# Local attention on one Trainium2 core: rotary partner rows fetched by DMA, 64-row score matmuls, and the exponentials of each head on ScalarE from PSUM

## The chip, the cores and the metric

The kernel runs as one launch on 1 core of one Trainium2 chip, all in float32. The metric is the device time of the launch in microseconds (us). The engines of the core are named PE (TensorE), ACT (ScalarE), DVE (VectorE), POOL (GpSimd) and SP (SyncE, which here only issues DMAs). Each runs its own list of instructions in order; the lists are tied together by semaphores only.

## The reference

The program is two transformer layers over x of shape (2, 2048, 128): local attention, a mixture of experts, causal attention and a second mixture of experts, each with a layer norm and a residual. Only the first stage is touched by the change:

```python
xn = rmsnorm(layernorm(x), norm_w)
q, k, v = split(xn @ w_qkv)              # 16 heads of 64
q, k = rope(q), rope(k)                  # x*cos + x_rot*sin; x_rot: (-x[odd], x[even]) of each pair
# segments of 64 tokens; 16 memory keys/values (pm_k, pm_v) are put before the 64 of the segment
scores = q_s @ k_s.T * 64**-0.5          # per head 64 x 80
scores = where(allowed, scores, min)     # memory, and causal inside the segment
attn = softmax(scores)
out = (attn @ v_s) @ w_out + b_out
x = x + layernorm(out)
```

## The kernel before, in words

The stage `local_attention` (L88) first loads x and the weights and splits every weight into a high float32r part `wh` and a low part `wl` (`matmul_split`, L62, computes a product as three matmuls: high·high at L64, high·low at L65, low·high at L66). The rotated weight columns (`rot`, the odd/even partners with their sign) are prepared once as weights of their own, so that the projection yields both x and x_rot.

The work is cut in 16 **steps** (`NSUB`). A step projects one block b of 256 tokens and at the same time attends over the block before, a, as two tiles of 128 tokens (s = 0, 1); the function `step` is written out for each engine, and the order of its lines is the order on that engine. A loop (`Fori`, L300) runs the middle steps in pairs. A last step has only the attention of the last block.

- PE, per step: values of b (`values_of`, four products of 512 columns, L64 to L66), then 16 column tiles ct (`project`, eight for q and eight for k, each with two products, one plain and one rotated, of 256 columns) in two PSUM banks `pbank`. Between them stand the scores of tile (a, 1) (`scores`, L535: per bank two mask matmuls at L542 and up to six pairs of 160 columns at L547; the keys of a head pair lie in one 160-column tile `kt` of 128 rows, with zeros where a head's rows meet the other's columns), and the **fills** of both tiles: seven PSUM fills per tile (`FILL`), transposes of the probabilities ("pt", L595) and products with the values ("ot", L603), alternating between two banks `fbank`, each copied out by ACT (L499). Then the output product (L616, L619). At the end of the step come the scores of tile (b, 0) and the transpose of the next block's input (`turn`, L529).
- ACT: four value copies (L506), one exponential per tile over all 16 heads, SBUF to SBUF (L490), the 14 fill copies (L499), the high part of the next input (`high`, L484).
- DVE: low part of the input (`low`, L322); per tile three maxima (L348), three subtractions of the maximum out of PSUM (L355), and after the exponential the sum (L363), its reciprocal (L365) and half of the normalising product (L369); 16 products with cos and sin straight from `pbank` (`rope`, L339), eight additions for the upper half of the keys (L330); the layer norm of the output (L376 to L391).
- POOL: the other additions of cos and sin part (L439 for q, L442 for k), the other half of the normalising product (L451, L454), a power per tile (L461).

What orders the stage are these lists and the waits in them: `project(ct)` waits until DVE has read tile ct-2 out of its bank, `scores` until DVE has subtracted in the bank, a fill until the normalised probabilities are there and until the bank's last copy is done.

## Time and profile before

| | |
|---|---|
| time, median of 3 runs | 2588.97 us (2580.05 to 2591.15) |
| profiled execution | 2589.86 us, its span 2588.0 us |
| granted clock of PE, mean over the span | 0.938 of full speed |
| busy: PE, PE weight loads, DVE, ACT, POOL | 87%, 66%, 67%, 36%, 17% of the span |
| local attention, in the trace | start to about 658 us |

The profile is one execution.
### The profile page before, as it was taken

How to read it: one execution, taken by the hardware profiler on the slowest of the kernel's cores; microseconds unless marked ns; L12 is line 12 of the kernel's file. 1: busy time of each engine (PE TensorE's matmuls, PEld its weight loads, DVE VectorE, ACT ScalarE, POOL GpSimd, SP SyncE). 2: the span in 40 equal slices, each digit the busy share in tenths (PEclk: the TensorE clock that was granted, in tenths of full speed). 3: DMA queues.
4: the chain of work that ended last, by engine and by line, in shares of the span. 5: the costliest groups of instructions: out<-in, count | busy, mean ns of one | idle time of the engine just before them, and what ended most of it. 6: DMA issues, size and time to landing. Idle time of an engine off the chain costs nothing. (4 is left out here: it accounts for less than half of the span.)

```text
span 2588.0 us, 42404 instructions
## 1 busy us (share of the span) xinstructions
PE 2258.5 (87%) x14360; PEld 1708.4 (66%) x14360; DVE 1726.0 (67%) x4490; ACT 930.4 (36%) x1496; POOL 452.8 (17%) x426
## 2 busy tenths in 40 slices
PE   4999999998499998999976887699778969999998
PEld 3878888887244443444445776488657867888887
DVE  6888888887666664666647777767677775453334
ACT  2333333333135453444442221223223324444443
POOL 4655655564200000000000000300020010000000
PEclk9999999999589998899988998799889979999999
DMA  3000000000100000000000000000000010000000
GB/s 120 2 1 0 0 0 0 0 1 1 34 1 1 1 1 1 1 1 1 1 0 1 0 0 14 26 1 1 2 1 1 1 75 1 4 8 4 4 4 8
DMA packets 14259, 20.85 MB, mean 8 GB/s; under 512 B 1984, under 2 KB 12864, under 8 KB 13376
## 3 DMA queue, kind: packets, MB, share of 16 engines
q1 hardware_dynamic: 14144, 19.37, 2.2%
q8 instruction: 66, 1.08, 0.2%
q14 instruction: 49, 0.40, 0.1%
HBM read 17.27 MB, written 2.10 MB: 7 GB/s over the span
## 5 line engine op out<-in xcount | busy, mean ns | idle before, releaser
L974 ACT ACTIVATE mb_pt<-mb_stb 128x1024 f32<-128x1024 f32 x256 | 248.2, 1023 | 235.7 <-PE mb_stb L1063 235.0
L880 DVE TENSOR_REDUCE mb_mxp<-mb_p1b 128x1 f32<-128x512 f32 x352 | 225.6, 682 | 91.9 <-PE mb_p1b L1047 91.9
L2233 PEld LDWEIGHTS md_bk<-md_w,md_a 128*128 128x128 f32 x2048 | 263.9, 192 | 27.9 <-ACT md_a L2080 4.8
L2233 PE MATMUL md_bk<-md_w,md_a 128*128 128x128 f32 x2048 | 268.0, 276 | 4.0 <-DVE md_acc L2177 2.7
L2080 ACT ACTIVATE md_a<-md_bk,md_b 128x512 f32<-128x512 f32 x256 | 175.5, 687 | 240.5 <-PE md_bk L66 240.2
L1073 PE MATMUL mb_pvb<-mb_pt,mb_v 128*33 128x512 f32 x1024 | 244.4, 599 | 0.0
L2177 DVE SCALAR_TENSOR_TENSOR md_acc<-md_bk,md_gate,md_acc 128x128 f32<-128x128 f32 x256 | 71.7, 343 | 232.0 <-PE md_bk L2233 231.8
L339 DVE TENSOR_TENSOR ma_tr<-ma_pbank,ma_cs 128x512 f32<-128x512 f32 x256 | 173.5, 688 | 70.4 <-PE ma_pbank L66 65.8
L64 PE MATMUL ma_pbank<-ma_xth,ma_wh 128*128 128x256 f32 x512 | 165.2, 323 | 3.9 <-DVE ma_tr L339 1.9
L1856 ACT ACTIVATE mc_p<-mc_sb,mc_nb 128x512 f32<-128x512 f32 (+3 forms) x160 | 97.9, 621 | 190.2 <-DVE mc_nb L1744 190.2
L499 ACT ACTIVATE ma_pt<-ma_fbank 128x512 f32<-128x512 f32 (+1 forms) x160 | 85.3, 553 | 211.2 <-PE ma_fbank L595 211.2
L1934 PE MATMUL mc_pv<-mc_v,mc_pt 128*128 128x128 f32 x1088 | 150.3, 282 | 11.5 <-DVE mc_pt L1793 11.3
L1934 PEld LDWEIGHTS mc_pv<-mc_v,mc_pt 128*128 128x128 f32 x1088 | 134.3, 192 | 22.9 <-DVE mc_pt L1793 18.5
L1063 PE MATMUL mb_stb<-mb_qs,mb_ks 98*128 98x512 f32 x512 | 145.5, 406 | 3.2 <-ACT mb_pt L974 1.6
L65 PE MATMUL ma_pbank<-ma_xth,ma_wl 128*128 128x256 f32 x512 | 143.2, 280 | 0.0
L66 PE MATMUL ma_pbank<-ma_xtl,ma_wh 128*128 128x256 f32 x512 | 143.1, 279 | 0.0
L1047 PE MATMUL mb_p1b<-mb_ks,mb_qs 96*128 96x512 f32 x352 | 137.2, 473 | 2.8 <-DVE mb_qs L873 2.8
L64 PE MATMUL md_bk<-md_nh,md_wh 128*128 x256 | 120.4, 470 | 15.1 <-DVE md_acc L2177 12.4
L1047 PEld LDWEIGHTS mb_p1b<-mb_ks,mb_qs 96*128 96x128 f32 x352 | 63.6, 200 | 104.0 <-DVE mb_mxp L880 84.8
L442 POOL TENSOR_TENSOR ma_kt<-ma_tr 64x256 f32<-64x256 f32 x128 | 118.5, 930 | 54.5 <-DVE ma_tr L339 54.3
L1063 PEld LDWEIGHTS mb_stb<-mb_qs,mb_ks 98*128 98x128 f32 x512 | 94.9, 192 | 48.9 <-issue 13.4
L1184 POOL TENSOR_TENSOR mb2a_r<-mb2a_sv,mb_half 128x16 f32<-128x16 f32 x2 | 5.8, 2898 | 681.5 <-DVE mb2a_sv L1213 681.5
(333 smaller groups left out, 4956.0 us busy)
## 6 DMA issues: line engine op xcount, KB each, us to landing
mg_X<-x SPq DMA_DIRECT2D x4, 512.0 KB, 10.7
ma_cs<-cs SPq DMA_DIRECT2D x1, 2048.0 KB, 10.1
mc_cs<-cs SPq DMA_DIRECT2D x1, 2048.0 KB, 7.9
md_raw<-d_w SPq DMA_DIRECT2D x1, 2048.0 KB, 7.4
md_w<-d_w SPq DMA_DIRECT2D x1, 2048.0 KB, 10.9
out<-mg_X SPq DMA_DIRECT2D x8, 256.0 KB, 2.3
ma_raw<-w_qkv SPq DMA_DIRECT2D x1, 1536.0 KB, 8.8
mb_r<-b_w SPq DMA_DIRECT2D x1, 1152.0 KB, 5.2
```

What stands on the lines that cost most here:

```text
L64: nc.tensor.matmul(out, lhs_hi, rhs_hi, start=start, stop=False)
L65: nc.tensor.matmul(out, lhs_lo, rhs_hi, start=False, stop=False)
L66: return nc.tensor.matmul(out, lhs_hi, rhs_lo, start=False, stop=stop)
L339: nc.vector.tensor_tensor(tr[:, ct % 4, :, :], pbank[:, ct % 2, :].rearrange("p (r c) -> p r c", r=2), cs[:, bass.ds(b.j, 1), :, :].rearra ...
L880: nc.vector.tensor_reduce(mxp[:, r // NCH, r % NCH:r % NCH + 1], pass_bank(r), AXX, ALU.max).then_inc(p1_max, 1)
L974: nc.scalar.activation(pt[:, i % RING, :, :], stb[:, 2 * (i % 2):2 * (i % 2) + 2, :], ACT.Exp, scale=float(SCALE_B)).then_inc(exp_done, 1)
L1047: nc.tensor.matmul(pass_bank(r), qs[V % 2][0:QROWS, hh, t * P:(t + 1) * P], ks[0:QROWS, c * BLK:(c + 1) * BLK], start=True, stop=True).the ...
L1063: last = nc.tensor.matmul(stb[:, 2 * (i % 2) + hh, :], ks[:, i * P:(i + 1) * P], qs[U % 2][:, hh, :], start=True, stop=True)
L1073: last = nc.tensor.matmul(pvb[64 * hh:64 * hh + DK + 1, :], v1[:, i, :], pt[:, i % RING, hh, :], start=(i == 0), stop=(i == KT - 1), skip_ ...
L1934: last = nc.tensor.matmul(pv[:, 0:D], pt[:, k % 2, a * P:(a + 1) * P], v[:, c * BPT + a, :], start=(c == 0 and a == 0), stop=(c == chunks[ ...
L2080: nc.scalar.activation(a[:, e % 2, c, :], ub[:, c, :], ACT.Gelu, bias=b1[:, e, c:c + 1]).then_inc(gelu, 1)
L2233: last = nc.tensor.matmul(db[:, e % 2, s * P:(s + 1) * P], a[:, e % 2, c, s * P:(s + 1) * P], w2[:, e, c, :], start=(c == 0), stop=(c == F ...
```

## The change

It rewrites the stage in these places:

1. **Rotary partners by DMA.** The rotated weights and their projections are gone: 8 groups of two plain column tiles per step remain (`project`). ACT copies each group from `pbank` to SBUF (`copy_out`), SP issues two DMAs per group that write each row's partner row (odd to even, even to odd) to `swp`, DVE multiplies the copy by cos (`cosine`) and the partner by a signed sin (`sine`), both from SBUF, and POOL adds two column tiles at once over all 128 rows (`add`).
2. **64-row scores.** The keys of a head lie on 64 rows with 80 columns. A score matmul has 64 rows, 64 columns of queries and 80 of keys; there are two groups (j = 0, 1) of 8 heads per tile in four PSUM banks, 4 mask matmuls and 16 score matmuls for each group.
3. **Exponentials.** DVE takes two negated maxima per tile (640 columns each); ACT computes each head's exponential straight from PSUM with the negated maximum as bias, 16 instructions of 80 columns per tile. The six subtractions are gone. The scale is folded into the q weights.
4. **Order.** The loop is written out, a tile's seven fills of s = 1 stand together behind the last projection, and `turn` and the output product share the two `fbank` banks, so `turn` is last in the step.

```diff
-            srcs = [(raw, 0, 0), (rot, 0, 2), (raw, 1024, 0), (rot, 1024, 0), (raw, 2048, 0)]
...
+            @block.sync
+            def _(sp):
+                for G in range(NSUB * NG):
+                    r = G % RAWS
+                    sp.wait_ge(raw_ready, G + 1)
+                    if G >= RAWS:
+                        sp.wait_ge(rope_sin, G - RAWS + 1)
+                    for i in range(2):
+                        sp.dma_start(swp[i:P:2, r, :, :], raw[1 - i:P:2, r, :, :]).then_inc(swapped[r], 16)
...
+                def cosine(b, i):
+                    G = b * NG + i
+                    dve.wait_ge(raw_ready, G + 1)
+                    if G >= TRS:
+                        dve.wait_ge(rope_add, G - TRS + 1)
+                    nc.vector.tensor_tensor(tr[:, G % TRS, 0, :, :], raw[:, G % RAWS, :, :],
+                                            cs[:, b // 2, 0, None, :].to_broadcast([P, 2, SUB]),
+                                            ALU.mult).then_inc(rope_cos, 1)
...
-                def tile_sub(a, s, b3):
...
+                def maxes(a, s, j):
+                    dve.wait_ge(s_mm, (a * ST + s) * QUADS + j + 1)
+                    nc.vector.tensor_reduce(mx[:, s, 8 * j:8 * j + 8].rearrange("p (b i) -> p b i", b=2), bank_of(j),
+                                            AXX, ALU.max, negate=True).then_inc(s_max, 1)
...
-                            nc.scalar.activation(e[:, s, :, :], e[:, s, :, :], ACT.Exp, scale=SCALE0).then_inc(exp_done, 1)
...
+                def exps(a, s):
+                    for j in range(QUADS):
+                        act.wait_ge(s_max, (a * ST + s) * QUADS + j + 1)
+                        for k in range(8):
+                            slot = 8 * j + k
+                            nc.scalar.activation(e[:, s, slot, :],
+                                                 sbank[:, 2 * j + k // 4, k % 4 * KEYS0:(k % 4 + 1) * KEYS0], ACT.Exp,
+                                                 bias=mx[:, s, slot:slot + 1]).then_inc(exp_done, 1)
...
+                    if live:
+                        values(b, 0, 1, 2, 3)
+                        copy_out(b, 0)
+                    if old:
+                        exps(a, 0)
+                    if live:
+                        copy_out(b, 1, 2)
+                    if old:
+                        exps(a, 1)
+                        evacuate(a, 0, 0, 1)
+                    if live:
+                        copy_out(b, 3)
+                    if old:
+                        evacuate(a, 0, 2, 3)
...
+                def scores(b, s, j):
+                    T = b * ST + s
+                    if T > 0:
+                        pe.wait_ge(exp_done, (T - 1) * H0 + 8 * j + 8)
+                    if s == 0:
+                        pe.wait_ge(rope_add, b * NG + (4 if j == 0 else 8))
...
+                    for i in range(4):
+                        for hf in range(2):
+                            q0 = s * P + 64 * hf
+                            for rg in range(2):
+                                rows, half = slice(64 * rg, 64 * rg + 64), slice(64 * hf, 64 * hf + 64)
+                                last = nc.tensor.matmul(sbank[half, 2 * j + rg, i * KEYS0:(i + 1) * KEYS0],
+                                                        qt[rows, par(b), 4 * j + i, q0:q0 + 64],
+                                                        kt[rows, par(b), 4 * j + i, 2 * s + hf, :],
+                                                        start=False, stop=True, skip_group_check=True)
```

How the instructions stand on three engines before and after (names: `ma_pbank` projections, `ma_qk` their copy in SBUF, `ma_swp` the partner rows, `ma_sbank` scores, `ma_e` exponentials, `ma_fbank` fills, `ma_pt`/`ma_ot` their copies).

ACT, the start of a step, before (second step of the program):

```order
L506 ACTIVATE ma_v<-ma_pbank 128x512 x4
L490 ACTIVATE ma_e<-ma_e 128x1280
L499 ACTIVATE ma_pt<-ma_fbank 128x512 x2
L490 ACTIVATE ma_e<-ma_e 128x1280
L499 ACTIVATE ma_ot<-ma_fbank 128x512
L499 ACTIVATE ma_pt<-ma_fbank 128x512 x2
```

and the same place in the changed kernel (third step):

```order
L501 ACTIVATE ma_v<-ma_pbank 128x512 x4
L511 ACTIVATE ma_qk<-ma_pbank 128x512
L483 ACTIVATE ma_e<-ma_sbank,ma_mx 128x80 x16
L511 ACTIVATE ma_qk<-ma_pbank 128x512 x2
L483 ACTIVATE ma_e<-ma_sbank,ma_mx 128x80 x16
L494 ACTIVATE ma_pt<-ma_fbank 128x512 x2
L511 ACTIVATE ma_qk<-ma_pbank 128x512
L494 ACTIVATE ma_ot<-ma_fbank 128x512
```

The first exponentials now stand behind a copy of the step's own projection, and the second 16 stand ahead of the first two fill copies, which in the kernel before stood ahead of the second exponential.

DVE, the start of a step, before:

```order
L322 TENSOR_TENSOR ma_xtl<-ma_misc,ma_xth 128x256
L348 TENSOR_REDUCE ma_mx<-ma_sbank 128x6 x2
L348 TENSOR_REDUCE ma_mx<-ma_sbank 128x4
L355 TENSOR_TENSOR ma_e<-ma_sbank,ma_mx 128x480 x2
L355 TENSOR_TENSOR ma_e<-ma_sbank,ma_mx 128x320
L339 TENSOR_TENSOR ma_tr<-ma_pbank,ma_cs 128x512
L363 TENSOR_REDUCE ma_den<-ma_e 128x16
L365 RECIPROCAL ma_rden<-ma_den 128x16
L369 TENSOR_TENSOR ma_pb<-ma_e,ma_rden 64x16x64
L339 TENSOR_TENSOR ma_tr<-ma_pbank,ma_cs 128x512 x4
```

and in the changed kernel:

```order
L314 TENSOR_TENSOR ma_xtl<-ma_fbank,ma_xth 128x256
L338 TENSOR_REDUCE ma_mx<-ma_sbank 128x8 x2
L322 TENSOR_TENSOR ma_tr<-ma_qk,ma_cs 128x512
L344 TENSOR_REDUCE ma_den<-ma_e 128x16
L346 RECIPROCAL ma_rden<-ma_den 128x16
L350 TENSOR_TENSOR ma_pb<-ma_e,ma_rden 64x16x64
L322 TENSOR_TENSOR ma_tr<-ma_qk,ma_cs 128x512
L329 TENSOR_TENSOR ma_tr<-ma_swp,ma_cs 128x512
L338 TENSOR_REDUCE ma_mx<-ma_sbank 128x8 x2
```

The sum and product of the first tile (L344 to L350) stand ahead of the maxima of the second (the last row), with one cosine and one sine between them.

PE, the end of a step in the changed kernel, behind the last projection:

```order
L623 MATMUL ma_fbank<-mg_ident,ma_pb 128x128 x8
L631 MATMUL ma_fbank<-ma_pt,ma_v 64x128 x8
L623 MATMUL ma_fbank<-mg_ident,ma_pb 128x128 x8
L631 MATMUL ma_fbank<-ma_pt,ma_v 64x128 x8
L623 MATMUL ma_fbank<-mg_ident,ma_ppm 128x128 x2
L640 MATMUL ma_fbank<-ma_wout,ma_ot 128x128 x8
L643 MATMUL ma_fbank<-ma_pmvw,ma_pt 128x128 x2
L593 MATMUL ma_sbank<-ma_mask,mg_identb 64x320 x4
L600 MATMUL ma_sbank<-ma_kt,ma_qt 64x80 x16
```

No projection is left between these fills; before, tiles 12 to 15 of `project` stood between them, and `turn` stood ahead of the last two score banks instead of behind all scores.

## Rows read from the trace of the kernel before

**Rows 1.** Busy us (instructions) by window: PE, PEld, DVE, ACT, POOL; then granted clock.
```profile
248.20:285.90 37.70, 36.05 (x328) 30.53 (x330) 31.06 (x58) 12.71 (x22) 21.29 (x22) 1.00 0.00 0
587.00:662.00 75.00, 56.73 (x526) 48.17 (x522) 48.70 (x109) 22.63 (x37) 29.56 (x30) 0.93 0.03 7
```
**Rows 2.** Timeline of ACT: L484 ten steps apart, two fill copies. Start us, us.
```profile
97.66 0.38 ACT L484 ACTIVATE ma_xth<-ma_misc 128x256 fp32r<-128x256 f32 x1 [3.48 <-PE ma_misc L529]
...
262.19 1.09 ACT L499 ACTIVATE ma_pt<-ma_fbank 128x512 f32<-128x512 f32 x2 [7.14 <-PE ma_fbank L595]
...
474.16 0.38 ACT L484 ACTIVATE ma_xth<-ma_misc 128x256 fp32r<-128x256 f32 x1 [3.90 <-PE ma_misc L529]
```
**Rows 3.** Timeline of PE, start of a middle step.
```profile
249.94 0.50 PE L64 MATMUL ma_pbank<-ma_wh,ma_xth 128*128 128x512 f32 x1
...
253.25 0.39 PE L64 MATMUL ma_pbank<-ma_xth,ma_wh 128*128 128x256 f32 x1
...
254.15 0.39 PE L542 MATMUL ma_sbank<-ma_mask,mg_identb 128*64 128x480 bf16 x2
254.38 0.98 PE L547 MATMUL ma_sbank<-ma_kt,ma_qt 128*64 128x160 f32 x12
...
261.55 1.03 PE L595 MATMUL ma_fbank<-mg_ident,ma_pb 128*128 128x128 f32 x8
```
**Rows 4.** Timeline, end of a middle step: next input's high and low part.
```profile
285.88 0.38 ACT L484 ACTIVATE ma_xth<-ma_misc 128x256 fp32r<-128x256 f32 x1 [3.91 <-PE ma_misc L529]
...
286.34 0.42 DVE L322 TENSOR_TENSOR ma_xtl<-ma_misc,ma_xth 128x256 fp32r<-128x256 f32 x1
```
**Rows 5.** Groups by line and shape: count, busy us, mean ns.
```profile
L499 ACT ACTIVATE ma_pt<-ma_fbank 128x512 f32<-128x512 f32 x128 | 73.0, 596 | 195.8 <-PE ma_fbank L595 195.8
L499 ACT ACTIVATE ma_pt<-ma_fbank 128x256 f32<-128x256 f32 x32 | 12.3, 384 | 15.4 <-PE ma_fbank L595 15.4
L1856 ACT ACTIVATE mc_p<-mc_sb,mc_nb 128x512 f32<-128x512 f32 x112 | 75.9, 684 | 170.5 <-DVE mc_nb L1744 170.5
L348 DVE TENSOR_REDUCE ma_mx<-ma_sbank 128x6 f32<-128x480 f32 x64 | 38.9, 647 | 0.3 <-PE ma_sbank L547 0.3
L348 DVE TENSOR_REDUCE ma_mx<-ma_sbank 128x4 f32<-128x320 f32 x32 | 15.3, 480 | 0.0
```
**Rows 6.** Timeline, softmax of one tile on DVE and POOL in a middle step.
```profile
254.45 0.69 DVE L339 TENSOR_TENSOR ma_tr<-ma_pbank,ma_cs 128x512 f32<-128x512 f32 x1 [1.96 <-PE ma_pbank L66]
255.08 1.49 DVE L363 TENSOR_REDUCE ma_den<-ma_e 128x16 f32<-128x1280 f32 x1
...
256.89 1.22 DVE L369 TENSOR_TENSOR ma_pb<-ma_e,ma_rden 64x1024 f32<-64x1024 f32 x1
256.94 2.94 POOL L451 TENSOR_TENSOR ma_pb<-ma_e,ma_rden 64x1024 f32<-64x1024 f32 x1 [0.98 <-DVE ma_rden L365]
```
**Rows 7.** Timeline of the causal attention: DVE and POOL, both reading SBUF.
```profile
1640.97 1.30 POOL L1814 TENSOR_TENSOR mc_rp<-mc_tr 128x512 f32<-128x512 f32 x1 [0.68 <-DVE mc_tr L1704]
1640.99 1.83 DVE L1710 TENSOR_TENSOR mc_kql<-mc_rp,mc_kqh 128x512 fp32r<-128x512 f32 x1
...
1643.87 0.67 DVE L1710 TENSOR_TENSOR mc_kql<-mc_rp,mc_kqh 128x512 fp32r<-128x512 f32 x1
```
**Rows 8.** Timeline of PE, last step, which has no projections.
```profile
635.03 1.97 PE L595 MATMUL ma_fbank<-mg_ident,ma_pb 128*128 128x128 f32 x8 [4.76 <-POOL ma_ppm L454]
...
646.32 1.04 PE L595 MATMUL ma_fbank<-mg_ident,ma_pb 128*128 128x128 f32 x8
648.18 1.09 PE L603 MATMUL ma_fbank<-ma_pt,ma_v 128*64 128x128 f32 x16 [0.83 <-ACT ma_pt L499]
...
653.27 2.02 PE L616 MATMUL ma_misc<-ma_wout,ma_ot 128*128 128x128 f32 x16 [0.41 <-ACT ma_ot L499]
655.13 0.61 PE L619 MATMUL ma_misc<-ma_pmvw,ma_pt 128*128 128x128 f32 x4
```
**Rows 9.** DMA issues: KB each, median us from issue to landing.
```profile
mg_X<-x SPq DMA_DIRECT2D x4, 512.0 KB, 10.7
...
mc_wo<-c_wo SPq DMA_DIRECT2D x1, 128.0 KB, 2.4
```

More of the change, by code:

```diff
@@ L432, in _ @@
+                finish(NSUB - 1, 1)
             @block.gpsimd
             def _(pool):
[L434 to L465 removed]
@@ L516, in step @@
                         high(nxt)
-                high(Sub(0, 0))
-                steps(act, step)
             @block.tensor
@@ new lines, in project @@
+                def project(b, i):
+                    if i >= 2:
+                        pe.wait_ge(raw_ready, b * NG + i - 1)
+                    else:
+                        pe.wait_ge(v_copied, b * 2 * ST + 3 + i)
+                    kind, c = GROUPS[i]
+                    for half in range(2):
+                        w0 = (1024 if kind == "k" else 0) + (2 * c + half) * P
+                        last = matmul_split(nc, pbank[:, i % 2, half * SUB:(half + 1) * SUB], wh[:, w0:w0 + P],
+                                            wl[:, w0:w0 + P], xth[:, :], xtl[:, :])
+                    last.then_inc(proj_mm, 1)
@@ L585, in fill @@
+                    last.then_inc(s_mm, 1)
+                def fill(a, s, *fills):
+                    T = a * ST + s
+                    for i in fills:
                         kind, q = FILL[i]
-                        bank = fbank[:, (s * FILLS + i) % 2, :]
+                        bank = fbank[:, i % 2, :]
                         if i == 0:
@@ new lines, in _ @@
+                turn(0)
+                for b, a, nxt in steps:
+                    live, old = b is not None, a is not None
+                    if live:
+                        values_of(b)
+                        project(b, 0)
+                    if old:
+                        scores(a, 1, 0)
+                    if live:
+                        project(b, 1)
+                    if old:
+                        scores(a, 1, 1)
+                    if live:
+                        project(b, 2)
+                    if old:
+                        fill(a, 0, 0, 1)
+                    if live:
+                        project(b, 3)
+                    if old:
+                        fill(a, 0, 2, 3)
+                    if live:
+                        project(b, 4)
+                    if old:
+                        fill(a, 0, 4, 5)
+                    if live:
+                        project(b, 5)
+                    if old:
+                        fill(a, 0, 6)
+                    if live:
+                        project(b, 6)
+                    if old:
+                        out_project(a, 0)
+                    if live:
+                        project(b, 7)
+                    if old:
+                        fill(a, 1, *range(FILLS))
+                        out_project(a, 1)
+                    if live:
@@ L655, in step @@
                         scores(b, 0, 0)
-                    if nxt:
-                        if a:
-                            pe.wait_ge(y_read, (a.n + 1) * ST)
+                        scores(b, 0, 1)
+                    if nxt is not None:
                         turn(nxt)
-                    if b:
-                        scores(b, 0, 1)
-                        scores(b, 0, 2)
-                turn(Sub(0, 0))
-                steps(pe, step)
 class Stats:
```

543 lines of the change are left out of this document (240 added, 303 removed).

## The prediction

> **What bounds the kernel now.** I read the busy time by windows first. In one middle step of local attention PE is busy for 36.05 of 37.70 us at a granted clock of 1.00 (2.4 GHz); DVE for 31.06, POOL for 21.29, ACT for 12.71 [rows 1]. Two starts of the same ACT instruction ten steps apart, 97.66 and 474.16, give the step: 37.65 us [rows 2]. So the stage is bound by PE's work, and DVE, though 82% busy, ends second. Then the timeline of PE at the start of a step: values 3.3 us, one projection 0.9 us, a bank of scores about 1.15 us with its masks, and the first fill 11.6 us into the step without a wait [rows 3]: whatever softmax needs is hidden under six projections. Last the timeline of the final step, which has no projections: there the fills of a tile and its output product are a chain of PE and ACT in turns [rows 8].
>
> **What the work alone would give.** 8 of 16 projections go, about 0.8 us each in a stream: -6.4 us of PE per step. PE's list is then: values 3.3, projections 6.8, fills and output products 11.8, `turn` 0.4, scores 4 groups. A group is 32 records of matmuls with 64 columns of weights and 4 masks. The nearest row with the same weights is L603: 16 records in about 1.03 us, 64 ns each [rows 8]; L547 has 76 ns for 160 columns [rows 3]. With its two column halves running together, one such record holds its half for 152 ns, so 80 columns for 76 ns. Upper end, nothing overlapping: 32 x 76 ns + 0.5 for the masks = 2.9 us. Lower end, all four quarters at once: 32 x 19 ns + 0.2 = 0.8 us. I take 1.8 us, nearer to L603 (32 x 64 ns + 0.25 = 2.3). Then PE's work is 29.5 us, against 34.5 by the same count before. DVE loses the subtractions and upper-half additions; ACT gains. If work decided, the step would fall. I do not think it will, since the order of the lists makes a longer chain of waits than 37.65 us.
>
> The Trainium skill ("TensorE: Matmul & The Clock Gate", Part 3) says that matmuls in different row and column tiles run concurrently and that weight loads overlap them only where the row group differs. By that rule a group costs the 0.8 us of the lower end, and the chain below is 2.0 us shorter per step. No row here has matmuls on separate 64-row halves; L547 shows the column halves overlapping.
>
> **The chain of a middle step, from PE's first value product at 0.** Ends without and with the port conflict told below.
> - Values 3.3, projection 0 0.9 [rows 3], 0.3 until its result can be read (254.15 to 254.45) [rows 3, 6], copy by ACT 0.6 [rows 5]: 5.1 us.
> - 16 exponentials of tile 0. They are ready earlier (their maxima need only DVE at 0 to 1.6 us) but stand behind the copy on ACT. One: 596 ns for 512 columns and 384 for 256 give 0.83 ns a column, so 238 ns for 80, and 88 ns more for the bias from memory (684 against 596) [rows 5]; two in a row overlap by 0.10 us (1.09 for two) [rows 2]. So 226 ns each, 3.7 us: 8.8 us. Ends: 0.14 us each without the bias cost, 0.33 without overlap, that is -1.4 and +1.6 us per tile. One instruction of 1.27 us did this before.
> - Sum, reciprocal (1.81 us to the next) and half product 1.26 on DVE [rows 6]: 11.9 us. All 16 heads must be there.
> - One cosine and one sine, 0.60 each behind one another (0.67 recorded [rows 7]): 13.1 us; with the conflict 15.0.
> - First negated maximum of tile 1: 647 ns for 480 columns and 1.04 ns for each of 160 more [rows 5]: 0.8 us: 13.9 / 15.8.
> - 16 exponentials of tile 1: 3.7: 17.6 / 19.5. Behind them on ACT wait the two fill copies of tile 0, 1.1 us [rows 2]: 18.7 / 20.6. PE's fills 0 and 1 can be there from 14.3 us (POOL's product ends 2.94 + 0.6 after the reciprocal [rows 6]); PE does projection 3 and then has nothing.
> - From the second copy to the output product of tile 0: ot 1.05, pt 0.4, projection 0.85, 0.3 to its result, its copy 0.5, copy of pt 0.6, hop 0.1, ot 1.05, projection 0.8, pt 0.15, projection 0.8: 6.6 us: 25.3 / 27.2.
> - Output product 2.2 (653.27 to 655.13 and the last four records 0.36 behind), projection 7 0.8: 28.3 / 30.2.
> - Fills and output product of tile 1, now without projections between them: the last step before shows the same chain from 646.32 to 655.74, 9.4 us at full clock [rows 8]: 37.7 / 39.6.
> - Scores of the next tile, two groups: 3.6: 41.3 / 43.2. The additions of the last group, on POOL at about 37 to 40 us, are in time.
> - `turn` 0.4, then with nothing on PE behind it the high part on ACT and low part on DVE, 285.88 to 286.76 and hops, 1.05 [rows 4]: 42.75 / 44.65 us.
>
> **The port conflict.** In the causal attention a DVE product of two SBUF operands took 1.83 us where POOL had begun an addition from SBUF 0.02 us before it, and 0.67 us where it had not [rows 7]; the blocked one ended 0.55 us after POOL's. Before, `rope` read PSUM and ran freely; cosine and sine read two SBUF operands, 16 per step. The first cosine that counts is issued at 11.9 us, inside POOL's product of about 10.65 to 13.6 us, so it ends near 14.15 and the sine near 15.0: +1.9 us. Later conflicts fall beside PE's own work. I take the 1.9 in full; the other end is 0.
>
> The Trainium skill ("SBUF — State Buffer", Who interferes with whom) states this rule: a DVE instruction with two SBUF inputs and a GpSimd instruction that reads SBUF exclude one another for a whole instruction. By it the step is the second number, without it the first; the rows above agree with it.
>
> **The clock.** After 4.76 us of idle time PE did eight transposes in 1.97 us instead of 1.04, at the 1.2 GHz level, and the window of the last steps has 0.93 [rows 8, 1]. The changed step has idle times of about 2.8 us (the wait for the exponentials ahead of the scores), 1.5 and 2.4 to 4.3 us (ahead of ot). The work behind the last, 2.3 us on the chain, could double: 0 to +2.3 us, and a little at the other places. I take +1.0.
>
> **DMA.** 16 issues of 128 KB per step. A DMA of 128 KB landed 2.4 us after issue, four of 512 KB in a crowded queue 10.7 [rows 9]. The first sine is wanted 7 us after its copy, the last about 5: hidden below some 5 us, and at 10.7 each step would wait some 5 us more. I take 0.
>
> **The rest at nothing:** the subtractions and the key additions lay beside PE, so removing them gains nothing here; two weight parts fewer in the preparation lie beside the loading of constants; the first and the last step I leave as they are, within 3 us.
>
> **The sum.** 44.65 + 1.0 = 45.65 us per step, 8.0 more than 37.65. Fifteen steps have both halves: +120 us on the profiled 2589.9 (2588.0 of span and 1.9 around it), 2709.9, which stands 0.9 above the median of the runs shown. Forecast 2710 us.
>
> **Rivals.**
> - *The short chain* (score groups 0.8, no conflict, full clock): 42.75 - 2.0 = 40.75 us, +46 us, 2636. For it: the exponentials' overlap and column halves that run together. Against: rows 7. Still slower. With exponentials at 0.14 us the step would reach 38.0.
> - *The clock falls widely, or transfers arrive late*: 49 to 51 us a step, 2760 to 2790. For it: three idle times per step where there was none. Against: 29.5 us of work in 45.
> - *PE's work stays the bound*: if the waits on ACT and DVE overlap better than I walked them, the step is PE's 29.5 us and the 3.15 that step and count differed by before, 32.65 us: -75 us, 2514. It decides only where the chain falls below 37.65, that is where softmax of tile 0 is through before the fills are wanted and tile 1's exponentials don't hold up the fill copies. Against: the order on ACT is fixed in the lists.
> - *The parts cancel*: near 2589.
>
> Chances: forecast with its bounds 0.62, short chain 0.20, wide clock or late DMA 0.11, PE's work 0.05, cancelled 0.02. Slower by over 0.5% (13 us, about what a measurement of this kernel tells from no change) 0.93, within 0.03, faster 0.04. The range leaves out the faster cases and the far ends: 2645 to 2775 us, from a step of 41.3 to one of 50.
>
> **What would show it.** A step of 43 to 47 us between two high-part copies. ACT's exponentials about 0.23 us apart, 3.7 us per tile, and the two fill copies directly behind the second 16. PE waiting 2 us and more at L600's masks, at the first pt and at the first ot, the last ended by ACT. DVE's cosine at 1.2 to 1.9 us where POOL's product runs. About 9.4 us from the eight transposes to the end of the output product. PE's busy share below 75% and a granted clock below 1.00. It is wrong if the step is below 41 us, if the score groups take over 2.5 us, or if PE waits for the partner rows.

## The result and the profile after

The changed kernel takes 2690.9 us (median of 4 runs, 2689.8 to 2691.4), the kernel before beside it 2588.3; the ratio is 1.0401, 95% interval 1.0377 to 1.0425: slower by 102.6 us. The profiled execution has a span of 2688.6 us and a mean granted clock of 0.901, where it was 0.938. PE's busy share over the program fell from 87 to 81%. In the medians below one execution is left out, of E3, which took 3248.9 us at a granted clock of 0.63.

By windows, one middle step of the changed kernel in three parts and whole, then the window of the last steps (columns: us, busy time and instructions of each engine, granted clock, DMA share, GB/s):

```profile
core 0: us, PE busy (x) PEld busy (x) DVE busy (x) ACT busy (x) POOL busy (x), PEclk, DMA share, GB/s
422.11:431.40 9.29, 5.92 (x60) 4.30 (x60) 3.12 (x6) 6.82 (x22) 0.00 (x0) 0.99 0.07 28
431.40:449.19 17.79, 10.97 (x88) 9.34 (x87) 14.05 (x15) 8.67 (x26) 10.23 (x6) 0.62 0.12 45
449.19:466.50 17.31, 14.93 (x200) 13.08 (x200) 11.80 (x21) 6.56 (x13) 9.46 (x9) 1.00 0.16 62
422.11:466.50 44.39, 31.82 (x346) 26.72 (x346) 28.97 (x41) 22.05 (x60) 19.69 (x14) 0.85 0.13 48
587.00:662.00 75.00, 53.92 (x609) 45.07 (x608) 47.30 (x72) 35.23 (x97) 30.78 (x23) 0.85 0.12 45
```

These answer to [rows 1]. PE had 96% of the step to do; now it is busy 72%, and no other engine is nearer to full. For 17.8 us of the step PE runs mostly at the lower of its clock levels.

The start of each step on ACT (start, duration), which answers to [rows 2]:

```profile
66.50 0.38 ACT L476 ACTIVATE ma_xth<-ma_fbank 128x256 fp32r<-128x256 f32 x1 [13.40 <-PE ma_fbank L555]
688.34 0.38 ACT L476 ACTIVATE ma_xth<-ma_fbank 128x256 fp32r<-128x256 f32 x1 [4.18 <-PE ma_fbank L555]
```

Fourteen steps lie between them: 44.42 us each (43.98 to 45.76), 6.77 more than 37.65. Over fifteen steps that is 101.5 us. That this is nearly the whole of the 102.6 us is partly chance, as two more rows show, the start of the second step before and the last matmuls of the stage after:

```profile
59.62 0.38 ACT L484 ACTIVATE ma_xth<-ma_misc 128x256 fp32r<-128x256 f32 x1 [20.73 <-PE ma_misc L529]
...
762.24 0.61 PE L643 MATMUL ma_fbank<-ma_pmvw,ma_pt 128*128 128x128 f32 x4
```

Up to the second step the changed kernel has lost 6.9 us (66.50 against 59.62), about half in the preparation and half in the first step, and its stage ends at 762.85 where it ended at 655.74 [rows 8], 107.1 us later. The code behind the stage, which nobody changed, was 6.5 us shorter in this execution (to the end of the span 1925.8 us, before 1932.3). In the traces of the experiments it takes 1924 to 1930 us, so differences of a few us in it say nothing.

The timeline of PE in the step that starts at 423.06 (start, us, in brackets the idle time ahead and what ended it), against [rows 3, 8]:

```profile
423.06 0.47 PE L64 MATMUL ma_pbank<-ma_wh,ma_xth 128*128 128x512 f32 x1 [0.98 <-ACT ma_xth L476]
...
429.74 0.33 PE L593 MATMUL ma_sbank<-ma_mask,mg_identb 64*64 64x320 bf16 x4 [2.43 <-ACT ma_e L483]
429.90 0.72 PE L600 MATMUL ma_sbank<-ma_kt,ma_qt 64*64 64x80 f32 x32
...
431.83 1.28 PE L600 MATMUL ma_sbank<-ma_kt,ma_qt 64*64 64x80 f32 x32
...
437.33 1.25 PE L623 MATMUL ma_fbank<-mg_ident,ma_pb 128*128 128x128 f32 x8 [2.64 <-POOL ma_ppm L446]
...
443.26 1.98 PE L631 MATMUL ma_fbank<-ma_pt,ma_v 128*64 128x128 f32 x16 [3.40 <-ACT ma_pt L494]
...
451.98 1.95 PE L640 MATMUL ma_fbank<-ma_wout,ma_ot 128*128 128x128 f32 x16
...
454.92 1.03 PE L623 MATMUL ma_fbank<-mg_ident,ma_pb 128*128 128x128 f32 x8
...
464.26 0.33 PE L593 MATMUL ma_sbank<-ma_mask,mg_identb 64*64 64x320 bf16 x4
...
465.77 0.44 PE L555 MATMUL ma_fbank<-mg_ident,ma_xn 128*128 128x128 f32 x2
```

The three long waits stand at the three places foretold, each ended by ACT or POOL. ACT in the same step:

```profile
427.84 3.59 ACT L483 ACTIVATE ma_e<-ma_sbank,ma_mx 128x80 f32<-128x80 f32 x16
...
438.59 3.60 ACT L483 ACTIVATE ma_e<-ma_sbank,ma_mx 128x80 f32<-128x80 f32 x16 [3.27 <-DVE ma_mx L338]
441.96 1.20 ACT L494 ACTIVATE ma_pt<-ma_fbank 128x512 f32<-128x512 f32 x2
```

Both fill copies stand directly behind the second sixteen exponentials, though PE had the fills ready at 438.3. And DVE and POOL between the two sets, to be held against [rows 6, 7]:

```profile
431.46 1.49 DVE L344 TENSOR_REDUCE ma_den<-ma_e 128x16 f32<-128x1280 f32 x1 [2.79 <-ACT ma_e L483]
...
433.27 1.22 DVE L350 TENSOR_TENSOR ma_pb<-ma_e,ma_rden 64x1024 f32<-64x1024 f32 x1
434.52 2.28 DVE L322 TENSOR_TENSOR ma_tr<-ma_qk,ma_cs 128x512 f32<-128x512 f32 x1
436.72 1.10 DVE L329 TENSOR_TENSOR ma_tr<-ma_swp,ma_cs 128x512 f32<-128x512 f32 x1
437.75 1.54 DVE L338 TENSOR_REDUCE ma_mx<-ma_sbank 128x8 f32<-128x640 f32 x2
439.21 0.68 DVE L322 TENSOR_TENSOR ma_tr<-ma_qk,ma_cs 128x512 f32<-128x512 f32 x1
```
```profile
433.31 2.94 POOL L443 TENSOR_TENSOR ma_pb<-ma_e,ma_rden 64x1024 f32<-64x1024 f32 x1 [11.42 <-DVE ma_rden L346]
436.21 1.06 POOL L446 TENSOR_TENSOR ma_ppm<-ma_e,ma_rden 128x256 f32<-128x256 f32 x1
```

A cosine takes 2.28 us beside POOL's product, and the next one 0.68 us where POOL is idle; cosine and sine each end about 0.55 us behind a POOL instruction. Last, the DMA issues (KB each, median us to landing; [rows 9]):

```profile
ma_swp<-ma_qk SPq DMA_DIRECT2D x256, 128.0 KB, 2.0
```

### The profile page after: what moved, and what is told of

The parts are those of the page before. It is cut to its first block and busy times, and to the rows that moved or that the text cites. A ratio compares the mean times of both kernels' runs of the same rounds, so it can differ in the third digit from the quotient of the medians.

```text
span 2688.6 us, 42307 instructions
## 1 busy us (share of the span) xinstructions
PE 2182.4 (81%) x14680; PEld 1644.4 (61%) x14680; DVE 1693.4 (63%) x4231; ACT 1070.6 (40%) x2102; POOL 426.0 (16%) x297
## 5 line engine op out<-in xcount | busy, mean ns | idle before, releaser
L322 DVE TENSOR_TENSOR ma_tr<-ma_qk,ma_cs 128x512 f32<-128x512 f32 x128 | 139.4, 1089 | 118.5 <-ACT ma_qk L511 118.0
L631 PE MATMUL ma_fbank<-ma_pt,ma_v 128*64 128x128 f32 x1024 | 85.6, 318 | 85.6 <-ACT ma_pt L494 85.6
L623 PE MATMUL ma_fbank<-mg_ident,ma_pb 128*128 128x128 f32 x512 | 97.9, 338 | 56.2 <-POOL ma_ppm L446 54.6
L483 ACT ACTIVATE ma_e<-ma_sbank,ma_mx 128x80 f32<-128x80 f32 x512 | 114.9, 379 | 68.2 <-DVE ma_mx L338 68.2
L631 PEld LDWEIGHTS ma_fbank<-ma_pt,ma_v 128*64 128x64 f32 x1024 | 69.1, 160 | 101.9 <-ACT ma_pt L494 101.9
L443 POOL TENSOR_TENSOR ma_pb<-ma_e,ma_rden 64x1024 f32<-64x1024 f32 x32 | 94.0, 2936 | 190.9 <-DVE ma_rden L346 190.9
L1096 PEld LDWEIGHTS mb_pvb<-mb_pt,mb_v 128*33 128x33 f32 x1024 | 49.0, 110 | 113.5 <-issue 113.2
```

Of the source, the lines that this page charges most:

```text
L322: nc.vector.tensor_tensor(tr[:, G % TRS, 0, :, :], raw[:, G % RAWS, :, :], cs[:, b // 2, 0, None, :].to_broadcast([P, 2, SUB]), ALU.mult). ...
L483: nc.scalar.activation(e[:, s, slot, :], sbank[:, 2 * j + k // 4, k % 4 * KEYS0:(k % 4 + 1) * KEYS0], ACT.Exp, bias=mx[:, s, slot:slot + 1 ...
L631: last = nc.tensor.matmul(bank[64 * hh:64 * hh + 64, (pr % 4) * P:(pr % 4 + 1) * P], v[:, par(a), s, h * DH0:(h + 1) * DH0], pt[:, slot_of ...
L1096: last = nc.tensor.matmul(pvb[64 * hh:64 * hh + DK + 1, :], v1[:, i, :], pt[:, i % RING, hh, :], start=(i == 0), stop=(i == KT - 1), skip_ ...
```

## The experiments

All times are medians, each with its own runs of the kernel before (2588.2 to 2589.6). "Against the changed kernel" compares the two differences from before; one step is a fifteenth of it.

**E1: the maxima of tile 1 first.**

```diff
                         softmax_back(a, 0)
+                        for j in range(QUADS):
+                            maxes(a, 1, j)
                     if live:
                         cosine(b, 1)
                         sine(b, 0)
-                    if old:
-                        for j in range(QUADS):
-                            maxes(a, 1, j)
```

> Edit on the changed kernel: on DVE the two maxima of tile 1 stand right behind softmax_back of tile 0, ahead of cosine 1 and sine 0; nothing else moves. Theory (the step is the chain through ACT's and DVE's lists): the blocked cosine (2.28 us) and sine (1.10) leave the chain, tile 1's 16 exponentials begin 3.3 us earlier, the fill copies behind them too; step 44.4 -> 41.1 us, 15 steps, -49 us, about 2642. Rival (the step is set by PE's work at the lower clock, or by something later in the step): the fills move but the step does not, within 10 us of 2691.

Measured: 2631.6 us, ratio to before 1.0159 (1.0142 to 1.0176), 60 us off the changed kernel. Its second sixteen exponentials start 13.3 us behind the high-part copy (405.36 less 392.10), where 438.59 less 422.11 is 16.5: 3.2 us earlier, 3.3 expected.

```profile
392.10 0.38 ACT L474 ACTIVATE ma_xth<-ma_fbank 128x256 fp32r<-128x256 f32 x1 [4.19 <-PE ma_fbank L553]
...
405.36 3.59 ACT L481 ACTIVATE ma_e<-ma_sbank,ma_mx 128x80 f32<-128x80 f32 x16
408.72 1.20 ACT L492 ACTIVATE ma_pt<-ma_fbank 128x512 f32<-128x512 f32 x2
```

Two instructions moved on an engine that is 65% busy are worth more than half of the loss; that engine's order is on the chain. The gain is 10 us above the forecast. The granted clock of such a step rose too, from 0.85 to 0.92; that it makes up the rest is not shown.

**E2: POOL's normalising products made tiny.**

```diff
-                    nc.gpsimd.tensor_tensor(pb[0:64, s, :, 0:SEG], e[0:64, s, :, PM:KEYS0],
+                    n, k = (H0, SEG) if a == 0 else (1, 1)
+                    nc.gpsimd.tensor_tensor(pb[0:64, s, 0:n, 0:k], e[0:64, s, 0:n, PM:PM + k],
...
```

> Edit on the changed kernel: from the second block on POOL's two normalising products per tile are made over 1 element a row (the lower half of the probabilities and the memory part keep the values of the first block; this part of the computation is left out). Port-conflict theory: cosine 1 and sine 0 behind the half product take 0.7 us each and end 2.0 us earlier; step -2.0 us, -30 us, about 2661. Rival (cosine is slow by itself, or from the partner DMAs that write SBUF at the same time): cosine 1 stays at 2.3 us, the time within 8 us of 2691.

Measured: 2661.8 us, ratio 1.0277 (1.0260 to 1.0294), 30 us off, as the conflict theory said. The edit takes away POOL's reading, its arithmetic and its writing together, so it names the product and not the part of it that shuts DVE out. DVE at the same place:

```profile
419.86 0.70 DVE L322 TENSOR_TENSOR ma_tr<-ma_qk,ma_cs 128x512 f32<-128x512 f32 x1
420.49 0.68 DVE L329 TENSOR_TENSOR ma_tr<-ma_swp,ma_cs 128x512 f32<-128x512 f32 x1
421.09 1.54 DVE L338 TENSOR_REDUCE ma_mx<-ma_sbank 128x8 f32<-128x640 f32 x2
```

**E3: exponentials without bias.**

```diff
-                                                 sbank[:, 2 * j + k // 4, k % 4 * KEYS0:(k % 4 + 1) * KEYS0], ACT.Exp,
-                                                 bias=mx[:, s, slot:slot + 1]).then_inc(exp_done, 1)
+                                                 sbank[:, 2 * j + k // 4, k % 4 * KEYS0:(k % 4 + 1) * KEYS0], ACT.Exp).then_inc(exp_done, 1)
```

> Edit on the changed kernel: the exponentials read no bias (the subtraction of the maximum is left out; the wait for the maxima stays). Theory from L1856's 684 against 596 ns: each exponential takes 0.14 us instead of 0.224, 16 take 2.3 us instead of 3.6; both tiles' are on the chain, so step -2.7 us, -40 us, about 2651. Rival: the fixed cost of a small ACT instruction out of PSUM is what counts, 0.22 us stays, and the time is within 8 us of 2691.

Measured: 2641.2 us, ratio 1.0197 (1.0168 to 1.0227), 51 us off (expected 40).

```profile
400.02 2.18 ACT L483 ACTIVATE ma_e<-ma_sbank 128x80 f32<-128x80 f32 x16
```

16 take 2.18 us, 0.136 us each, against 3.59 and 0.224: the bias read from SBUF costs 0.088 us each, 1.4 us a tile. Both tiles together explain 42 of the 51 us (15 steps of 2.8); the rest is open, and the granted clock over the middle steps rose beside it, from 0.85 to 0.88.

**E4: no partner DMAs.**

```diff
-                    nc.vector.tensor_tensor(tr[:, G % TRS, 1, :, :], swp[:, G % RAWS, :, :],
+                    nc.vector.tensor_tensor(tr[:, G % TRS, 1, :, :], raw[:, G % RAWS, :, :],
...
-                        sp.dma_start(swp[i:P:2, r, :, :], raw[1 - i:P:2, r, :, :]).then_inc(swapped[r], 16)
+                    sp.sem_inc(swapped[r], 32)
```

> Edit on the changed kernel: SP issues no DMAs for partner rows, the sine reads the copied rows themselves (the rotation is left out). Theory (transfers are hidden: 2.0 us from issue to landing, first wanted 7 us after the copy): within 5 us of 2691. Rival (late transfers or their SBUF writes hold up DVE): the sines start earlier or run faster, step -1 us or more, below 2676.

Measured: 2689.9 us, ratio 1.0387 (1.0368 to 1.0406): no difference from the changed kernel that could be told. The blocked cosine is as slow without any transfer beside it:

```profile
431.58 2.28 DVE L321 TENSOR_TENSOR ma_tr<-ma_qk,ma_cs 128x512 f32<-128x512 f32 x1
```

So the transfers are not its cause, and E2 has shown that POOL's products are.

**E5: turn ahead of the last output product.**

```diff
                         fill(a, 1, *range(FILLS))
-                        out_project(a, 1)
-                    if live:
-                        scores(b, 0, 0)
-                        scores(b, 0, 1)
                     if nxt is not None:
                         turn(nxt)
+                    if old:
+                        out_project(a, 1)
+                    if live:
+                        scores(b, 0, 0)
+                        scores(b, 0, 1)
```

> Edit on the changed kernel: on PE the transposes of the next block (turn) stand ahead of the output product and the scores that end the step, so that high and low part are made beside them. Chain theory: the 0.98 us in which PE waits for the low part goes, and nearly all of turn's place; step -1.0 to -1.4 us, 15 steps, -15 to -21 us, about 2673. Rival (the next step's start is held by ACT or DVE anyway): within 8 us of 2691.

Measured: 2674.9 us, ratio 1.0329 (1.0308 to 1.0351), 16 us off: 1.07 us a step. The wait of 0.98 us for the low part is gone; a new one of 0.59 us stands ahead of `turn`:

```profile
406.47 0.44 PE L555 MATMUL ma_fbank<-mg_ident,ma_xn 128*128 128x128 f32 x2 [0.59 <-ACT ma_pt L494]
```

**E6 and E9: needless matmuls in PE's waits.** E6 fills the first two waits, E9 all three. The cut below is E6's, but for its last two lines, which only E9 has: `spin_p` is the same as `spin` into `pbank`. E9 also has `spin(a, 5)` at the second place.

```diff
+                def spin(a, n):
+                    pe.wait_ge(y_read, a * ST)
+                    for _ in range(n):
+                        for half in range(2):
+                            matmul_split(nc, fbank[:, 1, half * SUB:(half + 1) * SUB], wh[:, 0:P], wl[:, 0:P],
+                                         xth[:, :], xtl[:, :])
...
                         project(b, 0)
+                    if live and old and a > 0:
+                        spin(a, 3)
                     if old:
                         scores(a, 1, 0)
...
                         project(b, 2)
+                    if live and old and a > 0:
+                        spin(a, 3)
...
                         project(b, 3)
+                    if live and old and a > 0:
+                        spin_p(b, 4)
```

> Edit on the changed kernel: in the two waits of PE ahead of the scores and ahead of the first fill (2.4 and 2.6 us) it makes three needless projections each (36 more matmuls a step) into a free bank; the result is the same and nothing waits for them. Clock theory (the granted clock fell to the 1.2 GHz level about 2 us after the first wait and the work from the fills to the first output product took 8.9 us where 6.6 was walked at full clock): with PE busy the clock stays at 1.00 there, step -2 us or more, -30 us, about 2660, faster although PE does more. Rival (the clock follows something else, or that work waits on ACT at either clock): the time stays at 2691 or rises.

Measured: 2690.6 us, ratio 1.0390 (1.0373 to 1.0407): nothing. The forecast of 2660 missed. The level no longer fell at the scores, but it fell at the fills, where PE had still waited 1.92 us, and stayed down through the products with the values:

```profile
392.59 1.69 PE L623 MATMUL ma_fbank<-mg_ident,ma_pb 128*128 128x128 f32 x8 [1.92 <-POOL ma_ppm L446]
...
398.54 1.97 PE L631 MATMUL ma_fbank<-ma_pt,ma_v 128*64 128x128 f32 x16 [2.98 <-ACT ma_pt L494]
```

So the null result left two readings open: that the clock costs nothing, or that the costly part was still slow. E9 was made to tell them apart.

> As e6, with five needless projections instead of three ahead of the first fill and four more (into the free projection bank) ahead of the first product with the values, where e6 still had PE idle for 1.9 and 3.0 us and the granted clock fell there: 72 needless matmuls a step. Clock theory: now the level stays at 2.4 GHz through the fills of tile 0; the eight projections and fills there take half the time they took, step -1 to -2.3 us, 2656 to 2676. Rival (the part between the fill copies and the output product waits for ACT's copies at either clock, and e6's null result says that the clock costs nothing here): within 8 us of 2691, or above it because the added matmuls stand in the way.

Measured: 2670.7 us, ratio 1.0316 (1.0299 to 1.0333): 72 more matmuls a step, and 20 us faster. The granted clock is 1.00 for the whole step, and the products with the values take 1.09 us instead of 1.98:

```profile
408.74:451.32 42.58, 36.12 (x418) 31.46 (x418) 29.95 (x41) 21.83 (x59) 20.12 (x14) 1.00 0.13 50
```
```profile
428.62 1.21 ACT L494 ACTIVATE ma_pt<-ma_fbank 128x512 f32<-128x512 f32 x2
...
429.92 1.09 PE L631 MATMUL ma_fbank<-ma_pt,ma_v 128*64 128x128 f32 x16 [1.31 <-ACT ma_pt L494]
...
436.37 1.95 PE L640 MATMUL ma_fbank<-ma_wout,ma_ot 128*128 128x128 f32 x16
...
440.48 0.66 PE L623 MATMUL ma_fbank<-mg_ident,ma_pb 128*128 128x128 f32 x4 [0.57 <-DVE ma_y L357]
```

From the second fill copy (429.83) to the output product (436.37) lie 6.5 us, where the changed kernel has 8.8 (443.16 to 451.98): 2.3 us less. 0.7 us of it is lost again behind it, where the second fill of tile 1 now waits for DVE.

**E7: one exponential per group.** One shift is shared by eight heads, which softmax allows as long as no head's scores lie so far below the others' that its exponentials vanish; a general kernel would need a guard.

```diff
-                        for k in range(8):
-                            slot = 8 * j + k
-                            nc.scalar.activation(e[:, s, slot, :],
-                                                 sbank[:, 2 * j + k // 4, k % 4 * KEYS0:(k % 4 + 1) * KEYS0], ACT.Exp,
-                                                 bias=mx[:, s, slot:slot + 1]).then_inc(exp_done, 1)
+                        nc.scalar.activation(e[:, s, 8 * j:8 * j + 8, :].rearrange("p (b i) k -> p b (i k)", b=2),
+                                             sbank[:, 2 * j:2 * j + 2, 0:QW], ACT.Exp,
+                                             bias=mx[:, s, j:j + 1]).then_inc(exp_done, 1)
```

> Edit on the changed kernel, order unchanged: one negated maximum over the 8 heads of a group and one exponential of 640 columns per group instead of 8 of 80 (4 per step instead of 32). Chain theory: 16 exponentials of 3.6 us become two of about 0.7 each, -2.2 us for each tile, both on the chain; step -4.4 us, -65 us, about 2626. Rival (only one of the two tiles is on the chain, the other is covered): -2.2 us a step, about 2658.

Measured: 2611.9 us, ratio 1.0087 (1.0070 to 1.0103), 79 us off (expected 65). The maxima are one for each group then, in an edit of the same kind that is not shown.

```profile
384.18 1.47 ACT L482 ACTIVATE ma_e<-ma_sbank,ma_mx 128x640 f32<-128x640 f32 x2
```

1.47 us for a tile in place of 3.59, and both tiles pay: 2.1 us twice in 15 steps is 64 of the 79 us. The mean granted clock rose from 0.901 to 0.916 beside it; what it is worth here was not measured.

**E12: part 3 alone, in the kernel before.**

```diff
-                            act.wait_ge(s_sub, (a.n * ST + s + 1) * 3)
-                            nc.scalar.activation(e[:, s, :, :], e[:, s, :, :], ACT.Exp, scale=SCALE0).then_inc(exp_done, 1)
+                            for b3 in range(3):
+                                h0, nh = 2 * PAIRS_OF_BANK[b3][0], 2 * len(PAIRS_OF_BANK[b3])
+                                act.wait_ge(s_max, (a.n * ST + s) * 3 + b3 + 1)
+                                for k in range(nh):
+                                    nc.scalar.activation(e[:, s, h0 + k, :],
+                                                         sbank[:, b3, k * KEYS0:(k + 1) * KEYS0], ACT.Exp,
+                                                         bias=mx[:, s, h0 + k:h0 + k + 1]).then_inc(exp_done, 1)
...
-                        pe.wait_ge(s_sub, (T - 1) * 3 + b3 + 1)
+                        pe.wait_ge(exp_done, (T - 1) * H0 + (6, 12, 16)[b3])
```

> The kernel before with the change's third part alone: negated maxima, no subtractions, 32 exponentials of 80 columns per step out of PSUM with bias, scale folded into the q weights; projections, rotation and scores as before. Theory (small exponentials on the chain cost here too: the scores of tile 1 wait for the first six of them, about 1.2 us, and the first fill, which had no slack, comes 1.5 us later; DVE has 2.9 us less to do): step 37.65 -> 39.5 to 40.5, 2615 to 2635. Rival (six projections and DVE's saved subtractions cover it): within 8 us of 2589.

Measured: 2638.0 us, ratio 1.0191 (1.0174 to 1.0208): 50 us slower, just above the theory's range. DVE is spared six subtractions a step and the kernel loses, with twice the projections there as cover. PE:

```profile
398.89 0.39 PE L536 MATMUL ma_sbank<-ma_mask,mg_identb 128*64 128x480 bf16 x2 [1.04 <-ACT ma_e L482]
...
404.86 0.38 PE L64 MATMUL ma_pbank<-ma_xth,ma_wh 128*128 128x256 f32 x1 [1.05 <-DVE ma_tr L340]
```

The scores wait for the exponentials as expected. What had not been walked is the second wait: on DVE the sum stands ahead of the next `rope`, so the late exponentials hold up the projections too.

**E8, E10, E11: the lists in another order.** E8 has E7's edit, and PE's list, written short, reads as in the second line in place of the first (ACT, DVE and POOL follow it):

```
-  p2 F0.0 F0.1 p3 F0.2 F0.3 p4 F0.4 F0.5 p5 F0.6 p6 O0 p7 | F1.0 to F1.6 O1 | S0 S1 turn
+  p2 F0.0 F0.1 p3 F0.2 F0.3 F0.4 p4 F0.5 F0.6 p5 O0 F1.0 p6 F1.1 p7 F1.2 F1.3 F1.4 S0 F1.5 F1.6 turn O1 S1
```

(p projections, Fs.i fill i of tile s, O output product, S the next block's scores.) ACT makes tile 0's exponentials around the first value copy; on DVE tile 0's sum comes ahead of cosine 0, and the maxima of tile 1 come right behind it, on either side of cosine 0. The first fill waits for POOL's first product alone.

```diff
-                            pe.wait_ge(p_norm, T * 2 + 2)
+                            pe.wait_ge(p_norm, T * 2 + 1)
...
+                        if i == FILLS - 1:
+                            pe.wait_ge(p_norm, T * 2 + 2)
...
-                        fill(a, 1, *range(FILLS))
-                        out_project(a, 1)
+                        fill(a, 1, 2, 3, 4)
                     if live:
                         scores(b, 0, 0)
+                    if old:
+                        fill(a, 1, 5, 6)
+                    if nxt is not None:
+                        turn(nxt)
+                    if old:
+                        out_project(a, 1)
+                    if live:
                         scores(b, 0, 1)
-                    if nxt is not None:
-                        turn(nxt)
```

> The changed kernel with e7's edit and with the lists of PE, ACT, DVE and POOL written in another order: tile 0's exponentials and softmax_back at the step's start ahead of values and cosines, both maxima of tile 1 behind them, the first fill waits only for the first normalising product, projections 5 to 7 between the fills of tile 1, scores of the next block inside them, turn ahead of the last output product. Chain theory (the cost of the change is the order of the lists; its PE work is 29.5 us a step): step 31 to 33 us, 15 steps, about -180 us, 2490 to 2530, faster than the kernel before. Rival (the waits between engines that the change adds, copy, partner DMA, small exponentials, keep the step above 37.65 in any order): 2590 or above.

Measured: 2561.7 us, ratio 0.9897 (0.9874 to 0.9919): faster than the kernel before, but a step of 35.85 us in place of 31 to 33. PE's largest wait:

```profile
412.91 0.97 PE L625 MATMUL ma_fbank<-mg_ident,ma_pb 128*128 128x128 f32 x4 [3.61 <-DVE ma_y L358]
```

The fill waits until DVE has read the output product, and that read stands on DVE behind a cosine and three sines that ran beside POOL's instructions and took 2.28, 1.10, 1.77 and 1.75 us.

E10 is E8 without E7's edit:

> e8's order of the lists, but with the changed kernel's own 32 exponentials of 80 columns and maxima per head: the reordering alone. Theory: of the 2.2 us per tile that e7's edit saved, tile 0's stays on the chain (its exponentials stand between the value copies and hold values and sum up by 1.9 us) and tile 1's is partly covered; step 36 -> 38.5 us, about 2600. Rival (in the new order the exponentials are covered): 2562 to 2575. Other end (both in full): 40.5, about 2630.

Measured: 2601.7 us, ratio 1.0048 (1.0031 to 1.0065). With every instruction of the change kept, the order, with the wait of the first fill that goes with it, gives back 89 of the 102.6 us.

E11 moves two things in E8. The lines that they are moved from, and the second value copy, which goes ahead of an exponential, are not shown:

```diff
-                    rot((cosine, 3), (sine, 2), (cosine, 4), (sine, 3), (cosine, 5), (sine, 4))
+                    rot((cosine, 3), (sine, 2), (cosine, 4))
                     if old:
                         out_read(a, 0)
-                    rot((cosine, 6), (sine, 5))
+                    rot((sine, 3), (cosine, 5), (sine, 4), (cosine, 6), (sine, 5))
...
                     rot((sine, 7), )
+                    if live:
+                        maxes(b, 0, 0)
...
                         high(nxt)
+                    if live:
+                        exps(b, 0, 0)
```

> e8 with two moves. DVE reads the output product of tile 0 (out_read) behind cosine 4, not behind sine 4; in e8 PE waited 3.6 us for that read ahead of the second fill of tile 1. The first maximum and the first exponential of the next tile 0 are made at the end of the step before, so that the value copies aren't held up (1.3 us). Theory: step 35.9 -> 32 to 33 us, about 2510. Rival (DVE, with its products shut out by POOL's, is the bound, and a read moved forward only pushes the rotations back, which the scores at the step's end wait for): 2545 or above.

Measured: 2534.0 us, ratio 0.9786 (0.9770 to 0.9802), the fastest kernel here, 54 us below the kernel before; the theory's 2510 was too low again. Three steps by windows (the mean of thirteen is 34.2 us), and PE's wait that is left:

```profile
368.15:401.23 33.08, 27.29 (x348) 22.98 (x347) 30.51 (x42) 17.44 (x31) 21.90 (x15) 1.00 0.17 65
401.23:435.64 34.41, 28.62 (x348) 24.07 (x347) 30.51 (x42) 17.45 (x31) 21.91 (x15) 0.95 0.17 63
435.64:470.64 35.00, 29.43 (x348) 25.24 (x347) 30.51 (x42) 17.67 (x32) 21.91 (x15) 0.90 0.16 61
```
```profile
406.21 0.48 PE L594 MATMUL ma_sbank<-ma_mask,mg_identb 64*64 64x320 bf16 x4 [2.78 <-POOL ma_kt L426]
```

DVE is busy 30.5 of 33 to 35 us, more than PE: here the rival of E11's expectation is partly right, the rotations behind the moved read end later, and POOL's last addition with them.

## Why the prediction was right

The forecast was 2710 us in 2645 to 2775; 2690.9 came. The mechanism was the walked one; that the number came within 19 us is partly luck, since two terms were mis-sized in opposite directions. The step of the profile above against the walk (end of each link, us from the first value product; the walk's second number, with the port conflict):

| link | walked | in the trace |
|---|---|---|
| copy of group 0 done | 5.1 | 4.9 |
| 16 exponentials of tile 0 | 8.8 | 8.4 |
| sum, reciprocal, half product | 11.9 | 11.4 |
| cosine and sine | 15.0 | 14.8 |
| first maximum of tile 1 | 15.8 | 15.5 |
| 16 exponentials of tile 1 | 19.5 | 18.9 to 19.1 |
| two fill copies | 20.6 | 20.1 |
| output product of tile 0 begins | 27.2 | 28.9 |
| projection 7 done | 30.2 | 31.9 |
| fills and output product of tile 1 | 39.6 | 41.2 |
| two score groups | 43.2 | 42.7 |
| next step | 45.65 with the clock | 44.1 |

- **That the chain and not the work sets the step** is shown: E1, E5 and E10 change no instruction, only its place (E10 one wait too), and take off 60, 16 and 89 us, and E9 adds work and is faster.
- **The small exponentials.** Walked at 0.226 us each, they take 0.224; the bias part, taken from [rows 5], is 0.088 us in E3. E7 is worth 79 us, and the third part costs 50 alone in E12.
- **The port conflict.** 1.9 us was taken in full; cosine and sine took 3.3 us for the 1.2 they would take free, and E2 gives 2.0 us a step. The walk had only the cosine shut out; in the trace POOL's second product shut out the sine too. The Trainium skill ("SBUF — State Buffer", Who interferes with whom) was weighed there; by that rule the step is the walk's second number, and the trace agrees. E2 and E4 show that POOL's product decides and the transfers do not; no run tells POOL's reading from its writing.
- **Score groups: mis-sized.** 1.8 us was taken; one took 0.88 us from its first mask (429.74 to 430.62), two took 1.5 (464.26 to 465.77). That was the lower end, 0.8, and makes the step 2.1 us shorter than walked. I had chosen by L603 because it has the same 64 columns of weights, but it ran on all 128 rows and says little of how separate 64-row quarters run. The Trainium skill ("TensorE: Matmul & The Clock Gate", Part 3) has row and column tiles run concurrently; the trace agrees, within 0.08 us of that bound.
- **The clock: mis-sized the other way.** 1.0 us was taken of 0 to 2.3. From the second fill copy to the output product lay 8.8 us, where 6.6 was walked at full clock, and E9 has 6.5 there at 1.00: the lower level costs 2.3 us on that stretch, the upper end. E9's whole step of 42.58, against 44.34 over the same thirteen steps of the changed kernel, is only 1.8 us shorter, for the new wait of 0.57 us and with 72 more matmuls.
- **What adds up.** The step of the table is 1.5 us below 45.65: -2.1 by the scores, +1.2 by the clock, -0.5 by the links up to the fill copies, each a little shorter than walked, and -0.1 by tile 1. The mean of 44.42 stands 0.3 above it, since three of the fourteen steps took 45.4 to 45.8.
- **DMA at nothing:** right. E4 changes nothing, and in 128 sines DVE waited once, 1.0 us, for a partner row.
- **Fills and output product of tile 1:** 9.3 us where 9.4 was read from the last step before [rows 8].
- **The other parts at nothing:** not quite. The first and the last step together stayed within the 3 us allowed (+3.4 and, what is left of 107.1, about -1.3), but the preparation, taken as hidden beside the loads, took 3.5 us more. The code behind the stage, shorter by 6.5 us in this execution, hides it in the total.

"PE's work stays the bound" was given 0.05 for the lists as they are. E11 is at 2534, where that rival had 2514, but by another mechanism: DVE is busier there than PE, and with the score groups as measured PE's count is about 25.5 us and not 29.5. That the two numbers are close is chance.

Left open: why two of the fourteen steps took 45.76 us, 1.6 more than their neighbours, at a granted clock of 0.81 where theirs was 0.84 and 0.85; how much of E11's shortfall is POOL's exclusion of DVE, since E11 was not run with the products elsewhere; and what the rotary partners by DMA and the 64-row scores cost or save each by itself, since only the third part was run alone.

## What to carry to other kernels

Before work is taken from a bound engine, walk the lists of the others with the new instructions in them: the change removed 8 of 16 projections and lost, largely because sixteen small instructions stood twice in a step between two uses of one in-order engine (making them two gave back 79 us). A row of small ACT instructions costs more by their number and their bias than by their columns (eight of 80 took 1.86 us, one of 640 took 0.80); widen them. When a rewritten stage is slower and no engine is full, try the order first: it gave back 89 of 102.6 us here with every instruction kept.

## What the runs showed of the hardware

- Work that is thrown away can pay: 72 matmuls a step into PE's waits held the granted clock at 1.00 and saved 20 us (E9). Filling two of three waits (36 matmuls, granted clock 0.88) saved nothing (E6).
- A DVE product of two SBUF operands beside a POOL product of 2.94 us and one of 1.06 was shut out twice in a row: cosine 2.28, sine 1.10, each ending about 0.55 us behind POOL's. A maximum from PSUM ran at its usual 0.8 us beside the first of them (E8, POOL's product from 393.89 to 396.83), and the cosine behind it did not:

```profile
395.11 0.82 DVE L339 TENSOR_REDUCE ma_mx<-ma_sbank 128x1 f32<-128x640 f32 x1
395.96 1.42 DVE L323 TENSOR_TENSOR ma_tr<-ma_qk,ma_cs 128x512 f32<-128x512 f32 x1
```

- 32 records of score matmuls on separate 64-row quarters, 80 columns each, took 0.72 us at full clock and 1.28 where the level had just fallen to 1.2 GHz.
- One exponential of 640 columns over two PSUM banks with a bias took 0.80 us (E7); eight of 80 columns took 1.86 (E10).
